# Conditioned recurrence: the f32 tanh in a PSUM bank, the bias on 128 rows, two blocks per loop, one bank for transposes and layer sums

## What is computed

```python
# b = 2 sequences, t = 1024 steps, d = 256 channels, RANK = 8
ae = _layernorm(ada_emb, ln_g, ln_b)
h = jax.nn.gelu(ae @ w1 + b1, approximate=False)
xw = h @ w2 + b2                                   # -> x_a, x_b, each (b, 256, 8)
layer = base_layer[None, :, :] + jnp.einsum('bdr,bkr->bdk', x_a, x_b)
y = x + (x + jnp.einsum('btc,bco->bto', x, layer))
...
xW = jnp.einsum('ntd,dh->nth', y, Wx) + b
def step(prev_h, xw):                              # 1,024 times, one after the other
    next_h = jnp.tanh(prev_h @ Wh + xw)
    return (next_h, next_h)
out = y + h_t
```

## Time and profile before

| | us |
|---|---|
| median of 3 runs | 816.48 |
| lowest, highest | 816.26, 816.67 |
| the profiled execution, its own time | 815.04 |
| its span in the profile | 813.2 |
| PE, PEld busy in it | 756.9, 696.4 |
| ACT, DVE busy in it | 397.6, 258.7 |
| granted clock of TensorE | 1.00 |

### The profile page before, as it was taken

One profiled execution on the slowest core, in us unless ns is written; L12 is line 12 of the kernel. 1 busy time (PEld: TensorE's weight loads), 2 busy tenths in 40 slices (PEclk: granted clock), 3 DMA queues, 4 the chain that ended last, 5 costly groups with the idle time before them and its releaser, 6 DMA issues.

```text
span 813.2 us, 48323 instructions
## 1 busy us (share of the span) xinstructions
PE 756.9 (93%) x21105; PEld 696.4 (86%) x21105; DVE 258.7 (32%) x1411; ACT 397.6 (49%) x3092; POOL 6.2 (1%) x17
## 2 busy tenths in 40 slices
PE   5799999999999999999999999999999999999997
PEld 4688888888888888888888888888888888888885
DVE  6433323333333323332323332323332323332322
ACT  6344444444444444444444444444444444444444
POOL 3000000000000000000000000000000000000000
DMA  7000000000000000000000000000000000000000
GB/s 263 6 10 6 6 6 5 3 6 5 6 6 5 3 6 5 6 6 5 3 6 5 6 6 5 3 6 5 6 6 5 3 6 5 6 6 5 3 6 6
DMA packets 12100, 9.76 MB, mean 12 GB/s; under 512 B 1813, under 2 KB 11056, under 8 KB 12080
## 3 DMA queue, kind: packets, MB, share of 16 engines
q1 hardware_dynamic: 11984, 9.45, 4.0%
q0 software_dynamic: 96, 0.02, 0.0%
HBM read 7.36 MB, written 2.10 MB: 12 GB/s over the span
## 4 chain that ended last, share of the span: by engine, by line
PE 88%; ACT 5%; issue 3%; DMA 1%; SPq 1%; DVE 1%; DVEq 0%; another core or an unknown queue 0%
PE acc L312 45%; PE pre L312 15%; PE acc L295 9%; PE p_y L276 7%; ACT h_pre L452 5%; PE pre L295 5%; PE acc L292 2%; PE p_xo L271 2%; DMA x_in<-x_dram 1%; PE pre L292 1%; PE p_xo L266 1%; SPq L212 1%; PE p_y L409 0%; SPq L209 0%; DVE lay_s L675 0%
## 5 line engine op out<-in xcount | busy, mean ns | idle before, releaser
L312 PE MATMUL acc<-h_pre,wh_s 128*128 128x2 f16 x8192 | 496.5, 167 | 37.6 <-issue 6.9
L312 PEld LDWEIGHTS acc<-h_pre,wh_s 128*128 128x128 f16 x8192 | 378.8, 106 | 85.6 <-ACT h_pre L452 70.4
L452 ACT ACTIVATE h_pre<-pre 128x4 f16<-128x4 f32 x1023 | 177.6, 174 | 398.6 <-PE pre L312 398.6
L556 DVE TENSOR_TENSOR h_lo<-h_f,h_pre 128x4 f16<-128x4 f32 x1024 | 167.5, 164 | 535.3 <-ACT h_f L458 534.2
L312 PE MATMUL pre<-h_rnd,wh_s 128*128 128x2 f16 x4092 | 259.0, 167 | 0.0
L312 PE MATMUL acc<-h_lo,wh_s 128*128 128x2 f16 x4096 | 253.2, 166 | 0.0
L312 PEld LDWEIGHTS acc<-h_lo,wh_s 128*128 128x128 f16 x4096 | 189.2, 105 | 0.0
L312 PEld LDWEIGHTS pre<-h_rnd,wh_s 128*128 128x128 f16 x4092 | 187.5, 106 | 0.0
L458 ACT ACTIVATE h_f<-acc 128x4 f32<-128x4 f32 x1024 | 177.9, 174 | 0.6 <-PE acc L312 0.6
L460 ACT ACTIVATE h_rnd<-acc 128x4 f16<-128x4 f32 x1022 | 171.8, 168 | 0.0
L295 PE MATMUL acc<-y_s,wx_s 128*128 128x16 f16 x2048 | 113.6, 177 | 0.0
(11 more groups left out here) (76 smaller groups left out, 161.9 us busy)
## 6 DMA issues: line engine op xcount, KB each, us to landing
w_f<-w_dram SPq DMA_DIRECT2D x8, 512.0 KB, 9.4
x_in<-x_dram SPq DMA_DIRECT2D x32, 64.0 KB, 2.3
out_dram<-o_row SPq DMA_DIRECT2D x64, 32.0 KB, 1.9
w_f<-w_dram SPq DMA_DIRECT2D x1, 256.0 KB, 2.8
base_f<-base_dram SPq DMA_DIRECT2D x1, 256.0 KB, 11.2
wh_f<-wh_dram SPq DMA_DIRECT2D x1, 256.0 KB, 10.7
wx_f<-wx_dram SPq DMA_DIRECT2D x1, 256.0 KB, 10.6
cond_r<-cond_dram SPq DMA_DIRECT2D x1, 2.0 KB
```

Source lines behind the costliest of these rows:

```text
L312: return nc.tensor.matmul(dst[:, mo, :], wh_s[:, pw, ki, mo * P:(mo + 1) * P], h[:, par, ki, :], start=False, stop=True, skip_group_check= ...
L452: nc.scalar.activation(h_pre[:, n % 2].rearrange("p m b -> p (m b)"), src, func, scale=scale).then_inc(s_hpre[(n // HALF) % 2], 1)
L556: nc.vector.tensor_sub(h_lo[:, par].rearrange("p m b -> p (m b)"), h_f[:, slot, :], h_pre[:, par].rearrange("p m b -> p (m b)")).then_inc( ...
```

## The change

Five edits, of which the last follows from the first:

- `h_f` is written to a PSUM bank `p_f` instead of SBUF. VectorE reads it there for `h_lo`, and right behind that copies it to the SBUF tile `h_f` for `sum_out`. ScalarE may overwrite `p_f` only after that copy: it waits for a new semaphore `s_hkeep` with the wait it already has. At the end of the program one more copy stands ahead of the last `sum_out`.
- `b_w` and `ones` have 128 rows; rows 3 to 127 of `b_w` are zero (one more GpSimd memset ahead of the loop).
- The loops hold two blocks each and go round 15 times. SP's loop stays as it is.
- Fillers are placed anew: input products in shares of 8 at u=2 to 8 of half A and of 7 at u=7 to 14 of half B; 28 layer products in half A from u=9 in shares of 5, four in half B at u=0; `turn_x` at u=5, `turn_out` of half B at u=2; VectorE's splits of `x` at u=6 and 7, of `y` at u=1, 2 and 5. No filler stands at u=15.
- `p_xo` and `p_y` become one bank, `p_w`, which frees the bank for `p_f`. Ahead of the loop, `pre[B]` serves in place of `p_y`.

```diff
-        b_w = sb("b_w", [3, D], F16)
-        ones = sb("ones", [3, HALF * NB], F16)
+        b_w = sb("b_w", [P, D], F16)
+        ones = sb("ones", [P, HALF * NB], F16)
...
-        p_xo = pb("p_xo", [P, 512])
-        p_y = pb("p_y", [P, 512])
+        p_w = pb("p_w", [P, 512])
+        p_f = pb("p_f", [P, 512])
...
-            EARLY, LATE = LAYER[:12], LAYER[12:]
+            EARLY, LATE = LAYER[:28], LAYER[28:]
...
-                    if 2 <= u < 10:
-                        input_products(B, share(INPUT, 7, u - 2))
+                    if 2 <= u < 9:
+                        input_products(B, share(INPUT, 8, u - 2))
                     if last:
                         continue
-                    if u == 10:
+                    if u == 5:
                         turn_x()
-                    if u == 13:
+                    if u == 9:
                         take(pe, s_xsplit, 1)
-                    if u >= 13:
-                        layer_products(share(EARLY, 4, u - 13))
+                    if 9 <= u < HALF - 1:
+                        layer_products(share(EARLY, 5, u - 9))
...
                     if u == 0:
-                        layer_products(share(LATE, 5, 0))
-                    if 2 <= u < 5:
-                        product = layer_products(share(LATE, 5, u - 1))
-                    if u == 4:
-                        product.then_inc(s_ymm, 1)
-                    if u == 9:
+                        layer_products(LATE).then_inc(s_ymm, 1)
+                    if u == 7:
                         take(pe, s_ysplit, 1)
-                    if u >= 9:
-                        input_products(A, share(INPUT, 8, u - 9))
+                    if 7 <= u < HALF - 1:
+                        input_products(A, share(INPUT, 7, u - 7))
...
-                nc.scalar.activation(h_f[:, (n - 1) % BLOCK, :], src, func, scale=scale).then_inc(s_hf[half], 1)
+                nc.scalar.activation(p_f[:, 0:COLS], src, func, scale=scale).then_inc(s_hf[half], 1)
...
+                    act.wait_ge(s_hkeep[half], u + 1)
                     act.wait_ge(s_sum[half], u + 1)
...
-            with act.Fori(0, NBLOCK - 1):
-                half_block(B)
-                half_block(A)
+            with act.Fori(0, (NBLOCK - 2) // 2):
+                for _ in range(2):
+                    half_block(B)
+                    half_block(A)
+            half_block(B)
+            half_block(A)
...
-                nc.vector.tensor_sub(h_lo[:, par].rearrange("p m b -> p (m b)"), h_f[:, slot, :],
+                nc.vector.tensor_sub(h_lo[:, par].rearrange("p m b -> p (m b)"), p_f[:, 0:COLS],
                                      h_pre[:, par].rearrange("p m b -> p (m b)")).then_inc(s_hlo[half], 1)
+                nc.vector.tensor_copy(h_f[:, slot, :], p_f[:, 0:COLS]).then_inc(s_hkeep[half], 1)
...
                         if u == 0:
+                            dve.wait_ge(s_hkeep[A], 1)
                             sum_out(B)
```

More of the change, by code:

```diff
@@ L242, in _ @@
             nc.gpsimd.memset(ones[:, :], 1.0).then_inc(s_ones, 1)
+            nc.gpsimd.memset(b_w[:, :], 0.0).then_inc(s_ones, 1)
             pool.wait_ge(s_ident, 2)
@@ L258, in _ @@
             step(5, nc.gpsimd.tensor_sub(b_parts[:, 2, :], b_rest[:, :], b_parts[:, 1, :]))
-            pool.dma_start(b_w[:, :], b_parts[0:1, :, :]).then_inc(s_bw, 16)
+            pool.wait_ge(s_ones, 2)
+            pool.dma_start(b_w[0:3, :], b_parts[0:1, :, :]).then_inc(s_bw, 16)
         @block.tensor
@@ L265, in turn_x @@
                 take(pe, s_xload, 16)
-                nc.tensor.transpose(p_xo[:, 0:P], x_in[:, :], ident[:, :]).then_inc(s_xturn, 1)
+                nc.tensor.transpose(p_w[:, 0:P], x_in[:, :], ident[:, :]).then_inc(s_xturn, 1)
             def turn_out():
                 take(pe, s_osum, 1)
-                nc.tensor.transpose(p_xo[0:HALF * COLS, 0:P], o_sum[:, :], ident[:, :]).then_inc(s_oturn, 1)
+                nc.tensor.transpose(p_w[0:HALF * COLS, 0:P], o_sum[:, :], ident[:, :]).then_inc(s_oturn, 1)
             def layer_products(todo):
-                py = p_y[:, 0:P].rearrange("p (t m b) -> p t m b", m=NM, b=NB)
+                py = p_w[:, P:2 * P].rearrange("p (t m b) -> p t m b", m=NM, b=NB)
                 for bb, mo, ki, pw, px in todo:
@@ L381, in _ @@
             for k in range(NM):
-                nc.tensor.transpose(p_xo[:, k * NB:(k + 1) * NB], cond_r[:, k * P:(k + 1) * P], ident[0:NB, 0:NB])
+                nc.tensor.transpose(p_w[:, k * NB:(k + 1) * NB], cond_r[:, k * P:(k + 1) * P], ident[0:NB, 0:NB])
             pe.wait_ge(s_vec, 48)
-            nc.tensor.transpose(p_xo[:, 64:64 + 3 * NM], vec_r[:, :], ident[0:3 * NM, 0:3 * NM]).then_inc(s_turn0, 1)
+            nc.tensor.transpose(p_w[:, 64:64 + 3 * NM], vec_r[:, :], ident[0:3 * NM, 0:3 * NM]).then_inc(s_turn0, 1)
             pe.wait_ge(s_norm, 1)
             for k in range(NM):
-                last = nc.tensor.transpose(p_y[:, k * NB:(k + 1) * NB], cond_n[:, k * P:(k + 1) * P],
+                last = nc.tensor.transpose(pre[B][:, k * NB:(k + 1) * NB], cond_n[:, k * P:(k + 1) * P],
                                            ident[0:NB, 0:NB])
@@ L394, in _ @@
                 for k in range(NM):
-                    last = nc.tensor.matmul(p_xo[:, 256 + mo * NB:256 + (mo + 1) * NB], w1_f[:, k, mo * P:(mo + 1) * P],
+                    last = nc.tensor.matmul(p_w[:, 256 + mo * NB:256 + (mo + 1) * NB], w1_f[:, k, mo * P:(mo + 1) * P],
                                             ae[:, k, :], start=k == 0, stop=k == NM - 1)
@@ L408, in _ @@
                         w = w2_s[:, pw, k, tile_of_ab(q)].rearrange("p (d r) -> p r d", r=RANK)
-                        last = nc.tensor.matmul(p_y[:, c:c + 2 * NB], w[:, r, :],
+                        last = nc.tensor.matmul(pre[B][:, c:c + 2 * NB], w[:, r, :],
                                                 hid_s[:, k].rearrange("p s b -> p (s b)"),
@@ L436, in _ @@
             pe.wait_ge(s_bw, 16)
-            pe.wait_ge(s_ones, 1)
+            pe.wait_ge(s_ones, 2)
             input_products(A, INPUT[:BEFORE])
             half_a(first=True)
-            with pe.Fori(0, NBLOCK - 2):
-                half_b()
-                half_a()
+            with pe.Fori(0, (NBLOCK - 2) // 2):
+                for _ in range(2):
+                    half_b()
+                    half_a()
             half_b()
@@ L474, in half_block @@
                 act.sem_clear(s_sum[half])
+                act.sem_clear(s_hkeep[half])
             act.wait_ge(s_var, 1)
@@ L483, in _ @@
                 for dst in (hid_s[:, m, 0, :], hid[:, m, :]):
-                    last = nc.scalar.activation(dst, p_xo[:, 256 + m * NB:256 + (m + 1) * NB], ACT.Gelu, bias=vec_c[:, 2, m:m + 1])
+                    last = nc.scalar.activation(dst, p_w[:, 256 + m * NB:256 + (m + 1) * NB], ACT.Gelu, bias=vec_c[:, 2, m:m + 1])
             last.then_inc(s_hidhi, 1)
@@ L580, in half_b @@
                     if u == 0:
+                        dve.wait_ge(s_hkeep[B], 1)
                         sum_out(A)
-                    if u == 3:
+                    if u == 4:
                         row_out()
@@ L585, in half_b @@
                         continue
-                    if u == 6:
+                    if u == 1:
                         finish_y()
-                    if u == 7:
+                    if u == 2:
                         split_y_high()
-                    if u == 8:
+                    if u == 5:
                         split_y_low()
@@ L622, in _ @@
             for k in range(NM):
-                last = nc.vector.tensor_scalar(ae[:, k, :], p_y[:, k * NB:(k + 1) * NB], vec_c[:, 0, k:k + 1],
+                last = nc.vector.tensor_scalar(ae[:, k, :], pre[B][:, k * NB:(k + 1) * NB], vec_c[:, 0, k:k + 1],
                                                vec_c[:, 1, k:k + 1], ALU.mult, ALU.add)
@@ L682, in _ @@
             half_a(first=True)
-            with dve.Fori(0, NBLOCK - 2):
-                half_b()
-                half_a()
+            with dve.Fori(0, (NBLOCK - 2) // 2):
+                for _ in range(2):
+                    half_b()
+                    half_a()
             half_b()
@@ L689, in _ @@
             dve.wait_ge(s_hf[A], 1)
+            nc.vector.tensor_copy(h_f[:, BLOCK - 1, :], p_f[:, 0:COLS]).then_inc(s_hkeep[A], 1)
+            dve.wait_ge(s_hkeep[A], 1)
             sum_out(B)
```

23 lines of the change are left out of this document (12 added, 11 removed).

## The result

The changed kernel takes 945.22 us (median; 944.28 to 946.69) against 816.37 of the kernel before in the same measurement: a ratio of 1.158 (95% interval 1.156 to 1.160). That is 129 us slower, outside the range.

The account below looks back on a forecast made before the run. It took the kernel as bound by 1,024 recurrence steps, chiefly on PE. Bias -18.0, branches -4.8, transpose +5.6, PSUM -3.6 and last copy +0.2 gave -20.6: 795.9 us forecast, range 785 to 848.

Parts of the forecast that it names:

- the next f32 tanh, which now waits for it, comes at 0.73: VectorE's copy of the f32 tanh: ends at 0.52, before the next tanh at 0.73; nothing counted, 2.5 us kept for range.
- PSUM by itself: f32 tanh written to PSUM, a shorter way to `h_lo`: 6 ns for 600 of 1,024 steps, 3.6 us gained.
- fifteen edges gained, 4.8 us: PE's loop branch with two blocks per loop: thirty edges become fifteen, 15 x 0.32 = 4.8 us gained.
- The rival: PE's code for the longer loop body no longer stays on the chip, so branches stall for fetches; chance 0.38.
- The bias: Bias products on 128 rows lose the gap around each pair: 6 x 0.10 x 31 blocks, taken as 18.0 us gained.
- The transpose: Transpose of `x` at u=5, behind eight input products, delays the next step by 0.18: 0.18 x 31 = 5.6 us lost.
- VectorE: Its 1,024 copies fit, even with the pair that takes `x` from PSUM at u=6; nothing taken, 2.5 us kept for range.
- The back edge: The step across PE's loop branch takes 1.05 us, 0.32 too long, once per turn of the loop.
- two of the three arrivals in a step are tied: PE being free, `h_rnd` and `h_lo` reach PE nearly together; neither f32 tanh nor `h_lo` holds the step by itself, about 0.01 us.

Follow-up runs that it names:

- a round of 1,707: Kernel before with bias on 128 rows, one block per loop and six idle PE products more behind each step of the loop: 1,014.93 us.
- one of 1,515: Kernel before with bias on 128 rows, one block per loop and three idle PE products more behind each step of the loop: 806.29 us.
- The hint: Changed kernel with its waits in the other order, plus a hint on PE naming the branch target each round: 865.33 us, against 886.62 without it.

## Why the prediction was wrong

It failed in two places, one of which it had as a rival.

*The new wait.* The step "the next f32 tanh, which now waits for it, comes at 0.73" counted the wait at nothing, because its signal is there early. The signal is early, as foreseen (copy done 0.42 after the tanh, tanh due at 0.73). What cost 0.06 per step was that the second wait took the place of the first on the tanh: the wait for the sum became an instruction of its own ahead of it. The working asked when the new signal comes and not what instruction carries each wait. Measured: 57 us, by the run with the order turned; in the other direction, PSUM by itself, 0 to 2 us lost where 3.6 were taken as gained.

*PE's code.* The step "fifteen edges gained, 4.8 us" assumed that 169 KB are held. The rival had the mechanism, its place and the 14 times; its price of 3.5 us was too low, since it had only the branch (4.02) and not the next piece of code, some 50 instructions further on, which stalls PE again (2.27 in the rows above). Together 6.3 a turn, net 79 us. I gave it 0.38. What held me back was that the kernel before contradicts the window of two pieces that the Trainium skill gives (Runtime: NRT & Kernel Launch, Instruction fetch mechanics). The other half of what that section says turned out nearer the truth, though not as a number: it gives PE 2048 instructions, and here a round of 1,707 isn't held and one of 1,515 is. Even alone either loss leads out of my range: 884 to 887 without the one, 864 without the other.

*The bias* was right in mechanism and size: 18.0 forecast, 18.6 measured. *The transpose* too: 5.6 forecast, 6.5 measured; it does hold PE for nearly the whole 0.27 (0.25 from 177.22 to the next MATMUL at 177.47). *VectorE* has room for its copies, as said: behind the pair that takes `x`, `h_lo` starts 0.19 after its tanh (0.20 in a plain step). All the same the next f32 tanh of that step (u=6) comes late in the kernels with `p_f`, by 0.10 in the changed kernel in every second block and by 0.02 to 0.04 with the waits turned, and not in the run with the tanh to SBUF. By the trace the signals of the sum and of the copy are both there then, and no row says what ScalarE waits for; the cause stays open (under 3 us in all). *The back edge* at 0.32 per turn was right: taking all 30 away gave 28.0 - 18.6 = 9.4 us, 0.31 each. And the sentence that two of the three arrivals in a step are tied, so that a faster `h_lo` is worth little, held: it is worth nothing.

## What to carry to other kernels

Before adding a wait to an instruction that already has one, see in the compiled program or the trace which of the two stands by itself, and let it be the one whose signal comes first; the late one belongs on the working instruction. In both orders tried here, the wait written last was the one that stood by itself. Before making a loop body longer, count its instructions per engine (a matmul is two) against the largest body that a trace shows going round without a fetch; if it won't fit, have no loop at all rather than a longer one. And a chain with three arrivals at the same moment gains nothing from one of them alone.

## What the runs showed that I had not expected

- A wait in an instruction of its own delays the next instruction of ScalarE by 0.06 us if it is the last to be satisfied, and by nothing if it is early (0.793 against 0.733 per step, the only difference being the order).
- A taken branch on PE to code that isn't held costs 3.3 to 4.5 us, and a second stall of 1.4 to 2.7 follows where the next piece begins, if that is near (52 to 84 instructions here). Each ends some 1.2 to 1.6 us after a piece of 16 KB has landed. The limit lies between 97 and 109 KB. The hint took 1.7 us off a branch.
- Straight code of PE, 166 pieces of 16 KB, costs nothing that shows.
- ScalarE's tanh of 128x4 takes 158 ns into PSUM and 174 into SBUF; VectorE's `h_lo` takes 162 ns with one input in PSUM and 164 with both in SBUF.
